# Attention block on one core: keys and queries as two float32r parts in row halves, and one ring of seven PSUM banks

## The reference

```python
def _L0_xattn_ref(tokens, context, Wq, Wk, Wv, Wo, bo):
    Q = _split_heads(tokens @ Wq)
    K = _split_heads(context @ Wk)
    V = _split_heads(context @ Wv)
    scores = jnp.einsum('bhnd,bhmd->bhnm', Q, K) * SCALE
    attn = jax.nn.softmax(scores, axis=-1)
    out = jnp.einsum('bhnm,bhmd->bhnd', attn, V)
    ...
    return out @ Wo + bo

def _L0_ffn_ref(x, w_gate, w_up, w_down):
    gate = fp4_linear(x, w_gate)
    y = fp4_linear(x, w_up)
    h = jax.nn.silu(gate) * y
    return fp4_linear(h, w_down)

x = x + _L0_xattn_ref(_layernorm(x, axis=-1), ctx_768, ...)
x = x + _L0_ffn_ref(_layernorm(x, axis=-1), ...)
```

## Time and profile before

| | before |
|---|---|
| median of three runs | 3501.74 us (3499.99 to 3502.39) |
| span of the profiled execution | 3497.6 us |
| PE busy | 3402.9 us, 97% |
| DVE busy | 2900.8 us, 83% |
| ACT busy | 2299.7 us, 66% |
| POOL busy | 1001.4 us, 29% |
| scores run | from 73.3 to 3425.7 us of the span |

### The profile page before, as it was taken

How to read it: one execution, slowest core, us unless ns; L and a number is a source line. 1 busy time by engine, 2 the same in 40 slices (tenths; PEclk the granted TensorE clock), 3 DMA queues, 4 the chain that set the end, 5 groups by cost and what they waited for, 6 DMA issues and landing times.

```text
span 3497.6 us, 55854 instructions
## 1 busy us (share of the span) xinstructions
PE 3402.9 (97%) x19606; PEld 1557.8 (45%) x19606; DVE 2900.8 (83%) x6561; ACT 2299.7 (66%) x4512; POOL 1001.4 (29%) x1114
## 2 busy tenths in 40 slices
PE   6999999999999999999999999999999999999997
PEld 3334444444444444444444444444444444444434
DVE  6878888888888988888888888988888888888865
ACT  2667666666666667666667666666666666666662
POOL 1323322333222323222333322333222333222213
PEclk8999999999999999999999999999999999999999
DMA  4333233232233332233232232332232231332310
GB/s 85 55 51 50 36 55 54 30 63 41 44 51 46 52 45 47 39 58 49 36 63 34 49 54 36 62 45 42 44 58 44 41 62 30 52 54 32 42 24 8
DMA packets 154262, 163.01 MB, mean 47 GB/s; under 512 B 58071, under 2 KB 127080, under 8 KB 153984
## 3 DMA queue, kind: packets, MB, share of 16 engines
q1 hardware_dynamic: 153984, 159.45, 28.9%
HBM read 46.22 MB, written 8.39 MB: 16 GB/s over the span
## 4 chain that ended last, share of the span: by engine, by line
PE 77%; DVE 17%; ACT 2%; POOL 1%; DMA 1%; issue 1%; SPq 1%; ACTq 0%; DVEq 0%
PE out_ps L912 19%; PE score_ps L901 18%; PE piece_ps L926 17%; DVE piece_max L1264 10%; PE work L865 6%; PE work L876 4%; PE work L832 3%; PE work L840 3%; ACT probs L1028 1%; PE work L821 1%; PE work L856 1%; PE work L873 1%; DVE ctx_T L1134 1%; PE work L850 1%; DVE stats L1107 1%
## 5 line engine op out<-in xcount | busy, mean ns | idle before, releaser
L1028 ACT ACTIVATE probs<-score_ps 128x512 f32<-128x512 f32 (+1 forms) x3328 | 1883.9, 600 | 900.0 <-PE score_ps L901 892.0
L1264 DVE TENSOR_REDUCE piece_max<-piece_ps 128x1 f32<-128x400 f32 (+1 forms) x4096 | 2113.3, 566 | 381.2 <-PE piece_ps L926 367.9
L926 PE MATMUL piece_ps<-k_stack,q_stack 96*128 96x400 bf16 (+1 forms) x4096 | 1291.3, 338 | 27.1 <-DVE piece_max L1264 12.6
L901 PE MATMUL score_ps<-q_stack,k_stack 99*128 99x512 bf16 (+1 forms) x3328 | 1251.7, 384 | 19.3 <-DMA q_stack<-neg_rows 5.2
L912 PE MATMUL out_ps<-probs,v_ones 128*17 128x512 f32 x6656 | 876.6, 599 | 0.4
L926 PEld LDWEIGHTS piece_ps<-k_stack,q_stack 96*128 96x128 bf16 x4096 | 385.1, 98 | 768.9 <-DVE piece_max L1264 514.7
L901 PEld LDWEIGHTS score_ps<-q_stack,k_stack 99*128 99x128 bf16 (+1 forms) x3328 | 324.2, 99 | 646.7 <-ACT probs L1028 494.5
L1316 POOL TENSOR_TENSOR h<-h,h_grid 128x704 f32<-128x704 f32 (+1 forms) x68 | 101.4, 1492 | 881.2 <-DVE h_grid L1092 881.2
L865 PE MATMUL work<-wgu_T,xq_T 128*128 128x512 f32 (+1 forms) x1080 | 333.8, 426 | 0.5
L912 PEld LDWEIGHTS out_ps<-probs,v_ones 128*17 128x17 f32 x6656 | 110.3, 95 | 270.3 <-issue 214.6
L865 PEld LDWEIGHTS work<-wgu_T,xq_T 128*128 128x128 f32 x1080 | 198.1, 191 | 44.0 <-issue 3.8
(11 more groups left out here) (170 smaller groups left out, 2711.4 us busy)
## 6 DMA issues: line engine op xcount, KB each, us to landing
k_stack<-k_parts SPq DMA_DIRECT2D x256, 150.1 KB, 3.6
k_stack<-k_parts SPq DMA_DIRECT2D x256, 100.1 KB, 3.9
ctx_in<-in_ctx SPq DMA_DIRECT2D x47, 384.0 KB, 3.7
k_stack<-k_parts SPq DMA_DIRECT2D x256, 50.0 KB, 3.7
q_stack<-q_parts SPq DMA_DIRECT2D x256, 48.0 KB, 2.8
x_in<-in_x SPq DMA_DIRECT2D x16, 512.0 KB, 5.0
q_stack<-q_parts SPq DMA_DIRECT2D x256, 32.0 KB, 2.1
resid<-in_x SPq DMA_DIRECT2D x62, 128.0 KB, 3.3
```

The costliest lines, as they stand in the source:

```text
L901: pe.matmul(score_ps[0:r, n % SCORE_RING, :], k_stack[:, par, slot(g, j), m * P:m * P + r], q_stack[:, par, slot(g, j), :], start=True, st ...
L926: pe.matmul(piece_ps[:, n % PIECE_RING, 0:hi - lo], q_stack[0:SROWS, par, slot(g, j), t * P:(t + 1) * P], k_stack[0:SROWS, par, slot(g, j) ...
L1028: act.activation(probs[0:r, step % 2, j, :], score_ps[0:r, (PER_GROUP * m + j) % SCORE_RING, :], ACT.Exp, scale=SCORE_SCALE).then_inc(prob ...
L1264: dve.tensor_reduce(piece_max[:, row, c:c + 1], piece_ps[:, n % PIECE_RING, 0:piece_at[c + 1] - piece_at[c]], AX_X, ALU.max).then_inc(piec ...
```

## The change

- **Parts.** Keys and queries are held as two float32r parts instead of three bf16 parts. Three products of parts remain (3 copies of 16 rows, `SROWS` = 48), and two rows carry the shift: 50 rows for a head.
- **Row halves.** Two heads of a group make a pair: one on partitions 0 to 49, the other on 64 to 113 of the same slot (`HALF` = 64). Their score matmuls, and their matmuls for the same piece, stand next to each other in the order and write different banks. The number of matmuls is the same; a piece now has 402 keys.
- **One ring.** Scores, pieces and rounds take their banks from one ring of seven in the order in which PE comes to them (`claim`): PE waits for whatever used the bank before, of whatever kind.
- **Merged readers.** Where both matmuls of a pair have adjacent banks, ACT takes one exponential over 1024 columns, and DVE one maximum over two banks. Over the whole program that is 1316 + 106 exponentials of two banks beside 440 + 44 of one, and 1749 maxima of two banks beside 598 of one; the wrap of the ring splits the others.
- **The order of a step** is fixed: `S01 P W01 P S23 P V` (scores of heads 0 and 1, a share of the pieces, all rounds of the step, pieces, scores 2 and 3, pieces, the weighted sum). The tables of places are other numbers.
- **Splitting.** ACT writes the first part and the whole, POOL subtracts once (before: three operations). `max_parts` has three operations instead of five. A head's stack takes four DMAs instead of six, with the same bytes; the shift takes four DMAs instead of one.

```diff
-STACK = [3, 2, 1]
-SROWS = sum(STACK) * HEAD_DIM
-SHIFT = 3
-SPLITS = 3
+SROWS = 3 * HEAD_DIM
+SHIFT = 2
+HALF = P // 2
+PAIRS = PER_GROUP // 2
+PAIR_SLOTS = 5
...
-    [4, 6, 6, 7, 9, 11, 16, 19, 19, 20, 22, 22, 23, 26, 29, 30, 34],
+    [4, 5, 5, 9, 13, 14, 19, 20, 20, 21, 23, 23, 23, 26, 33, 34, 38],
...
-SCORE_PLACE = [0.1225, 0.3125, 0.5225, 0.7625]
-PIECE_SHIFT = 0.8
+PIECES_AT = [
+    [3, 3, 4, 3, 2, 3, 3, 3, 3, 3, 2, 0, 0],
...
+STEP_ORDER = "S01 P W01 P S23 P V"
+RINGS, RING_FOR = (7,), (0, 0, 0)
+MERGE = (True, True)
...
+                step = g * KEY_TILES + m
+                left, slots = ahead * 2 * PIECES_AT[g][m], STEP_ORDER.count("P")
+                for what in STEP_ORDER.split():
+                    if what == "P":
+                        take = -(-left // (2 * slots)) * 2
+                        left, slots = left - take, slots - 1
+                        for _ in range(take):
+                            put(0, "piece", (g + 1) % PHASES, n)
+                            n += 1
+                    elif what[0] == "S":
+                        for j in what[1:]:
+                            put(NQ, "scores", step, int(j))
...
+    def merged(kind, batch, item):
+
+        if not MERGE[("scores", "piece").index(item[0])] or item[-1] % 2:
+            return False
+        at = PLACE[kind]
+        return at.get(partner(item)) == at[item] + 1 and bank(kind, batch, partner(item)) == bank(kind, batch, item) + 1
...
-        k_stack = sb("k_stack", [SROWS + SHIFT, 2, PER_GROUP + 1, KW], BF16)
-        q_stack = sb("q_stack", [SROWS + SHIFT, 2, PER_GROUP + 1, NQ], BF16)
+        k_stack = sb("k_stack", [P, PAIR_SLOTS, KW], F32R)
+        q_stack = sb("q_stack", [P, PAIR_SLOTS, NQ], F32R)
...
-        piece_ps = ps("piece_ps", [P, PIECE_RING, 512], F32)
-        score_ps = ps("score_ps", [P, SCORE_RING, 512], F32)
+        ring = ps("ring", [P, BANKS, 512], F32)
         out_ps = ps("out_ps", [P, 512], F32)
-        work_ps = ps("work", [P, 2, 512], F32)
...
+            def claim(kind, batch, item):
+
+                user = bank_user(kind, batch, item)
+                if user:
+                    pe.wait_ge(*released(*user))
...
-                if batch or g or n >= SCORE_RING:
-                    pe.wait_ge(probs_ready, count(batch, NSCORES * PHASES, NSCORES * g + banks_free(n, SCORE_RING, NSCORES)))
-                pe.matmul(score_ps[0:r, n % SCORE_RING, :], k_stack[:, par, slot(g, j), m * P:m * P + r],
-                          q_stack[:, par, slot(g, j), :], start=True, stop=True).then_inc(scores_ready, 1)
+                item = ("scores", step, j)
+                claim(kind, batch, item)
+                rows = slice(lo, lo + SROWS + SHIFT)
+                pe.matmul(ring[0:r, bank(kind, batch, item), :], k_stack[rows, at, m * P:m * P + r], q_stack[rows, at, :],
+                          start=True, stop=True).then_inc(scores_ready, 1)
...
+                rows, (a, b) = slice(lo, lo + SROWS), piece_at(c)
+                pe.matmul(ring[:, bank(kind, batch, item), 0:PW], q_stack[rows, at, t * P:(t + 1) * P], k_stack[rows, at, a:b],
+                          start=True, stop=True).then_inc(pieces_ready, 1)
...
-                    act.copy(rest[:, n % 2, 0:w], work[:, 0:w]).then_inc(this_drained, 1)
+                    act.copy(parts[:, 0, a:a + w].bitcast(F32R), work[:, 0:w])
+                    act.copy(parts[:, 1, a:a + w], work[:, 0:w]).then_inc(this_drained, 1)
...
+                act.activation(probs[0:r, step % 2, j:j + n, :], ring[0:r, at:at + n, :], ACT.Exp, scale=SCORE_SCALE).then_inc(probs_ready, n)
...
+                dve.tensor_reduce(piece_max[:, j:j + many, t, c], ring[:, at:at + many, 0:PW], AX_X, ALU.max).then_inc(pieces_max, many)
```

399 lines of the change are left out of this document (207 added, 192 removed), and 21 rows, old and new, of tables (PIECES_AT, PIECE_WEIGHT, POST_AT, TAIL_AT).

## The result

The changed kernel takes 3705.97 us (median of 4 runs, 3693.09 to 3720.70) against 3502.06 us before (3499.99 to 3506.84), a ratio of 1.0583 with a 95% interval of 1.0555 to 1.0611. It is 204 us slower; the prediction was 3145 us, 357 us faster. The profiled execution has a span of 3691.1 us.

The account below looks back on a forecast made before the run. PE and DVE, holding each other, were taken to bound the kernel. 63 groups at 47.0 (2961 us), a last group of 38, 71 before the first score, 72 after the last and 4 around gave 3145 us; 8-in-10 range 2980 to 3370.

Parts of the forecast that it names:

- the 1.4 us a group: Allowance per group for DVE's new stalls, about 3%, bringing 45.6 us to 47.0 us.
- Side by side: Scores and pieces on PE: pairs in row halves cost 0.236 and 0.22 us, saving 9.2 us a group.
- The rival that the halves run one after the other: Score and piece pairs on PE run serially, 55.4 us a group, 3680 us in all; chance 0.07.
- Changes of mode: PE switching between halves, full width and strips: 1235 more changes at 0.095 us, 117 us, 1.8 us a group.
- The bound of 0.12: Upper bound in us for one PE mode change, 148 us for all 1235 more.
- A load doesn't hide in a half: Rival: on PE a half's next weight load waits for its own matmul, 5.4 us more a group, 3350 us; chance 0.10.
- Merged maxima: DVE's maxima over two banks: 0.10 us gained for each of 1749 merged ones, 2.0 us less a group.
- What is late next. DVE: In the eleven steps with pieces DVE, at 39.8 us a group, is later than PE at 39.2.
- the two marks: Signs of being wrong: PE keeps three quarters of the chain, or scores wait for maxima over 200 us in total.
- The ring rival: Scores, pieces and rounds sharing one bank ring make scores wait for maxima, 4 us more a group, 3400 us; chance 0.13.
- The shift: Three more DMA issues late in a group might delay scores, a microsecond a group, 64 us; costed at nothing.

Follow-up runs that it names:

- e1: Changed kernel with both heads of a pair reading the same row half, so nothing runs side by side; 4568.63 us.
- e2: Changed kernel with scores and pieces reading all 128 rows, no row halves, shift left out; 3856.03 us.
- e7: Changed kernel without merged readers, one exponential and one maximum for each bank; 3552.26 us.
- e10: Changed kernel with only maxima merged, exponentials single; 3702.16 us.
- e15: Changed kernel without merging, but the bank of the first of two maxima is given back only with the second; 3654.64 us.
- e8: Changed kernel with scores reading 48 rows and not waiting for the shift, whose DMAs still run; 3634.60 us.
- e4: Changed kernel with separate rings of 2, 3 and 2 banks for scores, pieces and rounds instead of one of seven; 5033.11 us.
- e11: e7's kernel with the shift in two DMAs instead of four in four groups of five; 3488.75 us.
- e6: e2's kernel with scores and pieces reading rows 0 to 65 instead of all 128; 4009.49 us.
- e13: e11's kernel with scores reading 64 rows of each half instead of 50, the added rows zero; 3483.37 us.

## Why the prediction was wrong

The gain of the halves was forecast rightly. The terms that stand against it failed: the 1.4 us a group "for waits" (with a merged maximum costed as a gain), the changes of mode at 0.095 us, and the granted clock, which the sum doesn't have. The body was 544 us longer than forecast, 3543 us against 63 x 47.0 + 38 = 2999. The table has 519 of it: 267 us in stalls, 158 in changes and 140 in the lower clock, less 46 us that the halves saved beyond the forecast. The chance of 0.07 for "slower" stood for halves that run one after the other; it came out slower for other reasons.

**Side by side: right.** Halves start within 4 ns, pairs follow at 0.23 and 0.18 us (0.236 and 0.22 forecast), and work at its usual distance fell by 635 us (589 forecast). The rival that the halves run one after the other gave 3680 us and 55.4 us a group, which is what was measured (3706 and 55.4). That agreement is chance: e1 does run them one after the other, and takes over 4530 us. A time alone proves no mechanism.

**Changes of mode: a mis-sized term.** I had 1235 more changes at 0.095 us, 117 us; the trace has +275. The rule in the Trainium skill, "TensorEngine Tiling (Array Packing)", section "Key Properties", that a change of the tiling mode drains the engine, agrees with this case: 0.38 against 0.18 us behind rounds, and no extra there in e2, where rounds are no change. But the 0.10 of a bfloat16 change is half of the price. The 0.09 was read from bfloat16 operands; with float32 operands another 0.10 us stands at the first operation behind a change. The bound of 0.12 left this out, and no row of before could show it: there what follows a weighted sum is always a bfloat16 score or piece.

**A load doesn't hide in a half: wrong in general, right in one place.** In a run of halves it does hide (0.18 and 0.23 us for a pair with two loads). It seems exposed only in the first pair behind a change (0.10 us). The rule in the Trainium skill, "TensorE: Matmul & The Clock Gate", section "The mechanism" of Part 3, that a load overlaps a matmul in flight only when the row group differs, does not hold for loads within one mode here: e2 runs 128 rows at 0.185 us a piece (0.37 for two), each with a load of its own that is shown with 189 ns.

**Merged maxima: the sign was wrong.** The step was "a gain of 0.06 and of 0.10 us for each merged one", and DVE's busy time did fall: 2789.4 us with merging, 2874.8 without (e7), 2900.8 before. A double one is shown with 0.991 us (0.98 forecast), a double exponential with 1.026 (1.04). I costed the operation and not the bank that it holds. The loss is 150 us (e10), 102 of it by late release alone (e15).

**"What is late next. DVE": failed.** DVE is at 76%, not 86 to 88. With 39.8 us on DVE against 39.2 on PE I added 1.4 us a group for waits, 3%. When two engines need nearly the same time and hand banks to each other in strict order, waits are not a rest term: stalls grew by 395 us, 6.2 us a group. Merged maxima and the wait for the shift are two causes that runs show, worth 150 and 71 us of the kernel's time with the clock in them (e10, e8). Neither of the two marks I had set for being wrong was reached: scores wait for maxima for 163 us (under 200), and PE's share of the chain fell to 67% (under three quarters). A mark that one outcome and its opposite both pass is a poor one.

**The ring rival: not borne out.** Taking the common ring away makes it slower (e4, 5033 us, with merged readers). What the rival named, scores waiting for maxima behind one order, exists (163 us), and without merging it is as long (178 us in e7); what shrinks there are ACT's and DVE's waits for PE (by 212 and 184 us).

**The shift: named, and costed at nothing.** I put "a microsecond a group, 64 us" into the range and not into the sum. e8 measured 71 us; e11, with two issues fewer in four groups of five, won 64 us back on e7's kernel.

**The clock: not thought of.** The kernel before ran at a mean clock of 0.992. I took full clock for granted in a kernel that would have gaps, and lost 140 us to it in the body (186 us in the whole span). Here the granted clock goes down mostly behind gaps, and with 66 rows it did so more readily than with 128 (e2 against e6).

What stays open: how much of the clock's loss is due to rows and how much to gaps in the kernel after itself (e13 moved both little), the last 26 us of a merged maximum, and why even e11, without merging and with the shorter shift, is 344 us above the forecast; changes and clock are part of that. Stalls, changes and clock are not additive either: the run that takes away one cause shortens the others.

## What to carry to other kernels

Cost a merged operation by what it holds as well as by what it takes: half a microsecond's later release of one bank in seven cost more here than the merging saved. When the bounding engine's work is cut, write down its next waits (bank, reader, small DMA chain at a stage's start) with a time for each, and put them in the sum; where two engines come out within a few per cent of each other, three per cent for waits can be far too little (here the stalls grew by a tenth of the body). Packing into row halves pays in long runs of halves: count the changes of mode in a step, at some 0.2 us for a change into float32 operands, before counting the pairs.

## What the runs showed of the hardware

- Two float32r matmuls in different row halves start 4 ns apart and take the time of one (0.23 us for 512 columns, 0.18 for 402), with both weight loads hidden; in the same half they take 0.45 and 0.36 (e1).
- The first float32r operation behind a change of mode takes 0.19 to 0.20 us more, into halves from strips or from full width (0.43 against 0.23, 0.38 against 0.18) and into full width from strips (0.66 against 0.47 in e2); a bfloat16 one 0.10 (0.32 against 0.22 before).
- The same instructions in the same order, with nearly the same waits for the shift, had a mean granted clock of 0.988 when scores and pieces read 128 rows and of 0.937 with 66 (e2, e6).
- Zero rows added to a half moved the clock from 0.962 to 0.970, and the time not measurably (e13).
